# A decoder kernel: the heads' copy ahead of the exponentials, grouped loads at the opening, table products in two pairs, and two key and value units ahead of the barrier

## The reference, cut to what matters

```python
x = _layernorm(x + L0_attn(x))            # block-diagonal gates and a decaying scan
x = _layernorm(x + L0_xattn(x, ctx, ctx)) # retention: rotated q, k, a decay mask
x = _layernorm(x + L0_ffn(x))             # mixture of experts: 8 experts, top 2, 1024 slots each
x = _layernorm(x + L1_attn(x))            # causal self-attention, 2 heads of 128, rope, softmax
x = _layernorm(x + L1_xattn(x, ctx))      # 16 heads of 16 over ctx, with biases and a mask
x = _layernorm(x + L1_ffn(x))             # hashed experts, top 4 of 64

# L0_ffn: every token goes to its expert's slot and comes back by it
disp = disp.at[topi, pos_c].add(xk)
h = relu(einsum('ecm,emh->ech', disp, w1) + b1);  y = einsum('ech,ehm->ecm', h, w2) + b2
out = sum(gate[..., None] * y[topi, pos_c], axis=1)

# L1_xattn: keys and values hang on ctx alone
K = key_value_input @ Wk + bk;  V = key_value_input @ Wv + bv
```

## Time and profile before

| | |
|---|---|
| median of 3 runs | 1661.8 us (1661.14 to 1669.12) |
| the profiled execution | 1667.65 us, span 1665.9 us |
| TensorE clock granted, mean | 0.977 |
| PE busy | 1527.8 us, 92% of the span |
| PE weight loads, beside it | 1364.2 us, 82% |
| DVE busy | 1140.6 us, 68% |
| ACT busy | 801.7 us, 48% |
| POOL busy | 578.7 us, 35% |
| bytes moved | 152.03 MB, mean 91 GB/s |

### The profile page before, as it was taken

The page is one execution under the profiler, slowest core; times in us unless marked ns, Lnnn a source line. Parts: engine busy times, 40 slices in busy tenths (PEclk is TensorE's granted clock), DMA queues, the critical chain, the costliest instruction groups (busy, mean ns, idle before and its releaser), DMA issues.

```text
span 1665.9 us, 34482 instructions
## 1 busy us (share of the span) xinstructions
PE 1527.8 (92%) x12806; PEld 1364.2 (82%) x12806; DVE 1140.6 (68%) x2334; ACT 801.7 (48%) x1527; POOL 578.7 (35%) x679
## 2 busy tenths in 40 slices
PE   3888898899999999788888699999989999999997
PEld 2677777799999999777777578888879999999997
DVE  3899987756655565146777358877867768676775
ACT  5777742244544455236666444545434444443443
POOL 2666651212112120047776211212104444343444
PEclk8999999899999999999999899999999999999999
DMA  5122253212323330152233132121134553635443
GB/s 188 64 77 76 70 189 115 83 39 89 96 95 101 101 102 26 49 200 74 77 91 96 65 124 77 53 78 53 53 73 93 104 121 83 123 85 110 97 92 72
DMA packets 118829, 152.03 MB, mean 91 GB/s; under 512 B 10330, under 2 KB 103716, under 8 KB 118180
## 3 DMA queue, kind: packets, MB, share of 16 engines
q1 hardware_dynamic: 111540, 129.75, 28.4%
q0 software_dynamic: 6144, 16.79, 3.6%
q10 hardware_dynamic: 1008, 3.67, 0.6%
HBM read 111.37 MB, written 38.80 MB: 90 GB/s over the span
## 4 chain that ended last, share of the span: by engine, by line
PE 29%; DVE 11%; issue 7%; DMA 5%; ACT 4%; SPq 1%; POOL 1%; DVEq 0%; ACTq 0%; POOLq 0%
PE psum L518 7%; PE psum L1788 4%; DMA arena_x<-wT_d 3%; PE psum L1772 3%; PE psum L485 3%; PE psum L493 2%; PE psum L1766 2%; DVE psum L2358 2%; PE psum L1749 2%; PE psum L1488 1%; ACT arena_y L1519 1%; DMA wT_d<-arena_w 1%; DVE C_st L437 1%; PE psum L477 1%; PE psum L1485 1%
## 5 line engine op out<-in xcount | busy, mean ns | idle before, releaser
L2129 POOL TENSOR_TENSOR d_g_parts<-arena_w,d_g_parts 128x512 fp32r<-128x512 f32 x128 | 167.8, 1311 | 248.6 <-ACT d_g_parts L2261 240.9
L518 PE MATMUL psum<-d_v_high,d_g_parts 128*128 128x256 f32 x1024 | 205.1, 284 | 4.0 <-POOL d_g_parts L2129 2.3
L518 PE MATMUL psum<-d_x_parts,d_v_high 128*128 128x256 f32 x1024 | 193.5, 287 | 1.7 <-DVE d_x_parts L513 1.7
L518 PE MATMUL psum<-m_w_high,m_h_parts 128*128 128x256 f32 x1024 | 188.0, 285 | 0.0
L1192 ACT ACTIVATE arena_x<-psum,b_e 128x512 f32<-128x512 f32 x128 | 88.2, 689 | 190.1 <-PE psum L518 90.7
L518 PEld LDWEIGHTS psum<-d_v_high,d_g_parts 128*128 128x128 f32 x1024 | 167.5, 190 | 6.5 <-POOL d_g_parts L2129 4.1
L1120 POOL DMA_INDIRECT arena_x<-x_d,slot_row x64 | 66.9, 1045 | 293.6 <-PE psum L1166 229.3
L518 PEld LDWEIGHTS psum<-d_x_parts,d_v_high 128*128 128x128 f32 x1024 | 159.0, 191 | 8.6 <-DVE arena_w L2364 4.1
L518 PE MATMUL psum<-m_xF_parts,m_w_high 128*128 128x512 f32 x512 | 160.2, 395 | 2.1 <-DVE m_xF_parts L513 2.1
L518 PEld LDWEIGHTS psum<-m_w_high,m_h_parts 128*128 128x128 f32 x1024 | 160.9, 192 | 0.0
L2261 ACT ACTIVATE d_g_parts<-arena_w 128x512 fp32r<-128x512 f32 x128 | 80.8, 631 | 153.3 <-DVE arena_w L2364 152.4
(11 more groups left out here) (279 smaller groups left out, 3694.0 us busy)
## 6 DMA issues: line engine op xcount, KB each, us to landing
arena_x<-wT_d SPq DMA_DIRECT2D x128, 256.0 KB, 6.4
arena_y<-in_L_ffn_w SPq DMA_DIRECT2D x16, 1024.0 KB, 7.9
x_d<-arena_x SPq DMA_DIRECT2D x32, 256.0 KB, 2.2
y_d<-arena_x SPq DMA_DIRECT2D x16, 512.0 KB, 9.0
arena_x<-kv_d SPq DMA_DIRECT2D x16, 512.0 KB, 3.3
kv_d<-arena_x SPq DMA_DIRECT2D x9, 512.0 KB, 3.0
arena_x<-in_x SPq DMA_DIRECT2D x16, 256.0 KB, 2.9
arena_x<-in_ctx SPq DMA_DIRECT2D x16, 256.0 KB, 3.2
```

Source lines behind the costliest of these rows:

```text
L518: ins = nc.tensor.matmul(dst, left[a_], right[b_], start=start and k == 0, stop=stop and k == 2, skip_group_check=True)
L2129: nc.gpsimd.tensor_tensor(K["gP"][:, s % 4, 1], K["g"][:, s % 2], K["gP"][:, s % 4, 0].bitcast(F32), ALU.subtract).then_inc(d_gl, 1)
```

## The change

1. **Opening.** SP issues first the identity (128 x 128 of the constants), then x of unit 0, the vectors and the mask, then eight of the diagonal blocks; ACT issues the other eight, ahead of its first table load; POOL issues the rest of the constants, the three weights and the routing weight, through its software queue. There are four semaphores instead of one: `s_const`, `s_diag`, `s_tables`, `s_weights`. DVE's chain to `ndecay` comes ahead of what A doesn't need at once; three operations that need tables go to DVE's step 2.
2. **Routing.** Parts 0 and 1 of the table products follow ctx unit 5, parts 2 and 3 unit 6 (before: 0 behind unit 5, 1 behind 6, 2 and 3 behind 7). `KV_FIRST` is 10 instead of 9: one unit more is projected there.
3. **The barrier and C's start.** Four of the six remaining ctx units are loaded during M. Two are projected behind M's last tile, ahead of the barrier (ACT copies them; their stores are issued behind it). Three are projected ahead of C's step 0, and the last in step 3.
4. **C.** The heads' copy stands ahead of the exponentials in `c_scalar`.

```diff
-        loads = [(const[:, :], a["constants"])]
+        loads, tables_in, weights_in = [], [(const[:, P:], a["constants"][:, P:])], []
...
-            loads.append((w[name][:, :, :], a[name].rearrange("(c p) n -> p c n", p=P)))
-        loads.append((w_route[:, :, :], a["L0_ffn_wg"].rearrange("(c p) n -> p c n", p=P)))
+            weights_in.append((w[name][:, :, :], a[name].rearrange("(c p) n -> p c n", p=P)))
+        weights_in.append((w_route[:, :, :], a["L0_ffn_wg"].rearrange("(c p) n -> p c n", p=P)))
         loads.append((mask_in[:, :], a["mask"]))
-        N_EARLY = len(loads) + len(diag)
+        N_EARLY = 1 + len(loads)
...
         def setup_sync(sp):
+            sp.dma_start(const[:, 0:P], a["constants"][:, 0:P]).then_inc(s_const, 16)
+            sp.dma_start(A["x"][:, 0], x_u[0]).then_inc(a_in[0], 16)
             for dst, src in loads:
                 sp.dma_start(dst, src).then_inc(s_const, 16)
             sp.wait_ge(s_zero, 1)
-            for dst, src in diag:
-                sp.dma_start(dst, src).then_inc(s_const, 16)
+            for dst, src in diag[::2]:
+                sp.dma_start(dst, src).then_inc(s_diag, 16)
 
         def setup_pool(pool):
             nc.gpsimd.memset(gate_w[:, :, :, :], 0.0).then_inc(s_zero, 1)
             nc.gpsimd.memset(pool_cell[:, :], 0.0).then_inc(s_pow, 1)
             nc.gpsimd.memset(minus_half[:, :, :], -0.5).then_inc(s_pow, 1)
             pool.wait_ge(s_pow, 2)
+            for dst, src in tables_in:
+                pool.dma_start(dst, src).then_inc(s_tables, 16)
+            for dst, src in weights_in:
+                pool.dma_start(dst, src).then_inc(s_weights, 16)
 
         def setup_scalar(act):
-
+            act.wait_ge(s_zero, 1)
+            for dst, src in diag[1::2]:
+                act.dma_start(dst, src).then_inc(s_diag, 16)
             act.wait_ge(s_vec, 1)
...
         def setup_vector(dve):
             dve.wait_ge(s_const, 16 * N_EARLY)
             nc.vector.tensor_scalar(mask_f[:, :], mask_in[:, :], -BIG, None, ALU.mult).then_inc(s_maskf, 1)
-            dve.wait_ge(s_maskT, 1)
-            nc.vector.tensor_copy(mask_key[:, :], bank(6)[:, 0:B]).then_inc(s_mask, 1)
             dve.wait_ge(s_vecT, 1)
             nc.vector.tensor_copy(vec[:, :], bank(7)[:, 0:VEC_ROWS]).then_inc(s_vec, 1)
             dve.wait_ge(s_vec, 1)
             nc.vector.tensor_scalar(hgate_b[:, :], vec[:, V_BIN:V_BIN + 4], 0.5, None, ALU.mult).then_inc(s_setup, 1)
+            nc.vector.tensor_scalar(ndecay[:, :], vec[:, V_A:V_A + 2], 0.0, MIN_DECAY, ALU.max,
+                                    ALU.add).then_inc(s_setup, 1)
+            dve.wait_ge(s_maskT, 1)
+            nc.vector.tensor_copy(mask_key[:, :], bank(6)[:, 0:B]).then_inc(s_mask, 1)
+            dve.wait_ge(s_act_setup, 3)
+            dve.wait_ge(s_setup, 2)
+            nc.vector.tensor_tensor(ndecay[:, :], ndecay[:, :], sp_tmp[:, 2, :], ALU.add).then_inc(s_setup, 1)
+            dve.wait_ge(s_setup, 3)
+            nc.vector.tensor_scalar(pdecay[:, :], ndecay[:, :], 0.5, None, ALU.mult).then_inc(s_setup, 1)
+            dve.wait_ge(s_setup, 4)
+            nc.vector.tensor_scalar(ndecay[:, :], ndecay[:, :], -0.5, None, ALU.mult).then_inc(s_setup, 1)
+            nc.vector.memset(mask_one[:, :], -BIG).then_inc(s_setup, 1)
+            nc.vector.tensor_copy(ident_bf[:, :], ident).then_inc(s_setup, 1)
+
+        def setup_tables(dve):
+            dve.wait_ge(s_tables, 16)
             nc.vector.tensor_scalar(kb_par[:, 0, :], vec[:, V_BK:V_BK + 2], table("even_heads"), None,
                                     ALU.mult).then_inc(s_setup, 1)
             nc.vector.tensor_scalar(kb_par[:, 1, :], vec[:, V_BK:V_BK + 2], table("odd_heads"), None,
                                     ALU.mult).then_inc(s_setup, 1)
-            nc.vector.tensor_scalar(ndecay[:, :], vec[:, V_A:V_A + 2], 0.0, MIN_DECAY, ALU.max,
-                                    ALU.add).then_inc(s_setup, 1)
-            nc.vector.tensor_copy(ident_bf[:, :], ident).then_inc(s_setup, 1)
             nc.vector.tensor_copy(causal_bf[:, :], table("causal")).then_inc(s_setup, 1)
-            nc.vector.memset(mask_one[:, :], -BIG).then_inc(s_setup, 1)
-            dve.wait_ge(s_act_setup, 3)
-            dve.wait_ge(s_setup, 4)
-            nc.vector.tensor_tensor(ndecay[:, :], ndecay[:, :], sp_tmp[:, 2, :], ALU.add).then_inc(s_setup, 1)
-            dve.wait_ge(s_setup, 8)
-            nc.vector.tensor_scalar(pdecay[:, :], ndecay[:, :], 0.5, None, ALU.mult).then_inc(s_setup, 1)
-            dve.wait_ge(s_setup, 9)
-            nc.vector.tensor_scalar(ndecay[:, :], ndecay[:, :], -0.5, None, ALU.mult).then_inc(s_setup, 1)
+
+        N_DECAY = 5
         N_SETUP = 10
...
+                if u0 and not (u0.fixed and u0.n == 0):
...
+                    if t.fixed and t.n == 1:
+                        pe.wait_ge(s_diag, 16 * len(diag))
...
+                    if t.fixed and t.n == 4:
+                        pe.wait_ge(s_weights, 16 * len(weights_in))
...
-            act.wait_ge(s_setup, N_SETUP)
+            act.wait_ge(s_setup, N_DECAY)
...
+                    setup_tables(dve)
...
+                        pool.wait_ge(s_tables, 16)
...
-        KV_FIRST = 9
+        KV_FIRST, KV_LAST, KV_AHEAD, KV_EMPTY = 10, 2, 4, 5
...
                 if n == 5:
                     r_slot_rows(pe, 0)
+                    r_slot_rows(pe, 1)
                 if n == 6:
-                    r_slot_rows(pe, 1)
-                if n == 7:
                     r_slot_rows(pe, 2)
...
+        KV["cF_ahead"] = arena_x.shaped(arena_x.tile[:, 18432:20480], [P, KV_AHEAD, NC_, T])
...
+                if t.fixed and t.n == TILES - 1:
+                    done(sp, m_yp, Unit(0, TILES - 3))
+                    for k in range(KV_AHEAD):
+                        sp.dma_start(KV["cF_ahead"][:, k].rearrange("p c t -> p (c t)"),
+                                     cF_d[KV_FIRST + k]).then_inc(kv_ahead, 16)
...
+        KV["kv_rest"] = arena_x.shaped(arena_x.tile[:, 13312:17408], [P, 4, 2, NC_ * T])
+        kl_p, kl_s = sem("kl_p"), sem("kl_s")
+
+        def kv_last_tensor(pe):
+            pe.wait_ge(kv_ahead, 16 * KV_AHEAD)
+            for k in range(KV_LAST):
+                project_features(bank(4 - 2 * k), "L1_xattn_Wk", KV["cF_ahead"][:, k])
+                project_rows(bank(5 - 2 * k), "L1_xattn_Wv", KV["cF_ahead"][:, k]).then_inc(kl_p, 1)
+
+        def kv_last_scalar(act):
+            for k in range(KV_LAST):
+                act.wait_ge(kl_p, k + 1)
+                for j in range(2):
+                    nc.scalar.activation(KV["kv_rest"][:, k, j], bank(4 - 2 * k + j), ACT.Copy).then_inc(kl_s, 1)
+
+        add("tensor", kv_last_tensor)
+        add("scalar", kv_last_scalar)
+
         def m_end(sp):
             for k in range(2):
                 sp.wait_ge(m_st[k], 16 * (TILES // 2))
+            sp.wait_ge(kl_s, 2 * KV_LAST)
...
+        def kv_rest_project(pe, k):
+            if k < KV_AHEAD:
+                src = KV["cF_ahead"][:, k]
+            else:
+                src = KV["cF_rest"][:, k - KV_AHEAD]
+                pe.wait_ge(kr_in[k - KV_AHEAD], 16)
+            done(pe, kr_s, Unit(0, k - KV_LAST - 2), 2)
+            project_features(bank(4 + 2 * (k % 2)), "L1_xattn_Wk", src)
+            project_rows(bank(5 + 2 * (k % 2)), "L1_xattn_Wv", src).then_inc(kr_p, 1)
+
+        def kv_rest_take(act, k):
+            act.wait_ge(kr_p, k - KV_LAST + 1)
+            landed4(act, kr_st, Unit(0, k - 4, 4))
+            for j in range(2):
+                nc.scalar.activation(KV["kv_rest"][:, k % 4, j], bank(4 + 2 * (k % 2) + j),
+                                     ACT.Copy).then_inc(kr_s, 1)
+            act.wait_ge(kr_s, 2 * (k - KV_LAST + 1))
+            kv_rest_store(act, k)
+
+        def kv_rest_store(act, k):
+            act.dma_start(kv_d[KV_FIRST + k], KV["kv_rest"][:, k % 4]).then_inc(kr_st[k % 4], 16)
 
         def c_sync(sp):
             def step(t):
-                if t.fixed and t.n < 2:
-                    for k in ((0, 1), range(2, KV_REST))[t.n]:
-                        kv_rest_load(sp, k)
+                if t.fixed and t.n == 2:
+                    for k in range(KV_REST - KV_AHEAD):
+                        sp.dma_start(KV["cF_rest"][:, k].rearrange("p c t -> p (c t)"),
...
         def c_tensor(pe):
-            kv_rest_tensor(pe)
+            for k in range(KV_LAST, KV_EMPTY):
+                kv_rest_project(pe, k)
...
+                if t.fixed and t.n == 3:
+                    for k in range(KV_EMPTY, KV_REST):
+                        kv_rest_project(pe, k)
+                    pe.wait_ge(kr_s, 2 * (KV_REST - KV_LAST))
...
         def c_scalar(act):
-            kv_rest_scalar(act)
+            for k in range(KV_LAST):
+                kv_rest_store(act, k)
+            for k in range(KV_LAST, KV_EMPTY):
+                kv_rest_take(act, k)
 
             def step(t):
```

(11 more changed lines are left out.)

33 lines of the change are left out of this document (7 added, 26 removed).

## The result

Measured together, 20 runs each: before 1671.46 us, after 1658.73 us (medians; one run of before took 8529 us, which moves no median); ratio 0.9935, 95% interval 0.9917 to 0.9954. That is some 11 us less by the ratio (12.7 between the medians) where 26 were forecast, and 1658.73 lies above the range of 1625 to 1649. The direction was right, the size less than half. The median of before was itself 10 us above the 1661.8 of the three runs shown first; where that comes from is told under "All together". On the base of 1661.8, on which the range stands, the ratio gives 1651.0, still above 1649.

A forecast was written before the change was run, and what follows sets the result against it. PE busy 92% of the span; DVE bounds phase A, with waits at the opening, M's start, C's start and C's rounds. Terms -7.8, -2.0, -6.1, -7.6, -2.8 sum to -26.3: median forecast 1635.5 us, range 1625 to 1649.

The forecast's parts named there:

- The opening: Kernel's start: fewer SP loads ahead of the diagonal blocks let PE start earlier, -7.8 us, bounds -8.7 and -5.
- the third rival: Opening: small loads land behind 2.2 MB of tables, PE starts at 12.2, saving 3 us instead of 7.8; chance 0.08.
- I take 7.3: Opening: PE's assumed start in us, 6.5 being the earliest, against 15.19 before.
- The slower rival: Opening: POOL writes the descriptors of five large loads itself and is slow; 1694 us at k = 4; chance 0.03.
- The routing: Routing and M's start: first turn 0.3 us later but at a higher clock, -2.0 us, bounds +0.6 and -3.2.
- My bound of +0.6: Routing and M's start: the slow end, in us, of the bounds on the -2.0 term.
- C's start: Barrier and C's start: ACT normalises 11.6 us earlier, less 5.5 for clock and step 3: -6.1 us, bounds -11 and -3.
- forecast +5.5: C's start, behind the normalising: +2.5 us for PE's lower clock and +3.0 for the sixth unit in step 3.
- The second rival: C's start gives nothing: barrier, step 3, clock and memory-bound gathers take the gain, 1641.6 us; chance 0.14.
- The rounds and the last round: C: the earlier heads' copy saves 0.69 us in each of 11 rounds, -7.6 us, and -2.8 in the last round.
- the new circle: C's rounds: the chain through q and values that bounds a round after the copy's move, 11.86 us against 12.55.
- The first rival: C's rounds don't get shorter, the circle still closing at 12.5 us: 1644.4 us; chance 0.16.

The follow-up runs named there:

- opening_held: Kernel before with the new opening alone, POOL issuing tables and weights only when all sixteen diagonal blocks have landed; ratio 0.9926.
- the six combined profiles: Changed kernel with POOL's loads held, table products in old places, two late ctx loads first, in four unit placings, two of them run twice; ratios to before 0.9825 to 0.9884.
- after_spaced: Changed kernel with the four parts of the table products in their old places; ratio to before 0.9917.
- copy_only: Kernel before with only the heads' copy moved ahead of the exponentials; ratio 0.9955.
- combined: Changed kernel with POOL's loads held until the diagonal blocks landed, table products in old places, two late ctx loads first; ratio to before 0.9884, run again 0.9840.
- the last four kernels: Changed kernel with loads held, old table-product places and early ctx loads, in four placings of the six units, on one chip; ratios to before 0.9825 to 0.9840.
- after_early_cF: Changed kernel with SP issuing the two late ctx loads of C's start first, in step 0; ratio to before 0.9899.

## Why the prediction was wrong

**The opening: a term mis-sized, by the third rival.** Forecast -7.8 with PE at 7.3; measured -3.1 in after and -3.6 to -5.3 in the five other profiles of this opening, with PE at 10.9 to 11.9. The step that failed is "I take 7.3": it counted issues and the landing of an undisturbed load. The rival that let the small loads come in behind 2.2 MB gave -3 and was right, in its mechanism too; I gave it 0.08. With the bytes held back the term is -8.7 in opening_held, -8.6 to -8.9 in five of the six combined profiles and -6.5 in one, so the rest of the working stands. The slower rival, POOL's own time, was far off: 0.75 us for a load, whatever its size here, where I had 6 us for five at the least.

**The routing: a wrong sign.** Forecast -2.0, measured +4.1. I moved part 1 of the table products directly behind part 0 and wrote the 0.9 us for which PE waits there, but asked of the clock only at M's start, where the change could help. At the new wait I put it at nothing. There the clock fell, and 5.1 us on PE came right where the extra unit had made PE the last to be ready: the turn followed ACT's copy (1.18 idle), not the gathers. My bound of +0.6 left that out. The rest of the term was sound: without the fall it is -1.5.

**C's start: a wait that I didn't look for.** Forecast -6.1. The 3.7 us for the barrier were right (gathers begin 10.4 us behind M's last sums, before 6.6, +3.8), and so was what comes behind the normalising: forecast +5.5, measured 36.9 - 30.3 = 6.6. Wrong was "ACT is free (three units of PE end at 717.5), so it normalises" at 722.2: five units need five loads, four were ahead, and the fifth was queued on SP behind 1 MB of others. It was at 729.4. That the first mix came 1.5 us later than I had it is the rest. This part of the loss varies, too: the same kernel had 64.9, and after_spaced, with the load in the same place, 62.6. And the placing itself is worth little. Two ahead of the barrier and one in step 3 give 63.5, 62.7 and 62.7 us where the loads are first, all six at C's start 64.7, 62.0 and 62.7. The old placing gives 67.1 to 68.9 in seven profiles. The one unit that moved to the routing, 3.46 us, can be most of that difference; that is an estimate, since no run moves it alone, nor the four loads that are now issued in M. The second rival, "C's start gives nothing", had the right outcome for this kernel, but a late load was not among its reasons.

**The rounds and the last round: right.** 12.55 to 11.81 us, as the new circle said (11.86), and -12.2 for all of C's rounds where -7.6 - 2.8 = -10.4 were forecast: the 11 rounds gained 8.1, and what stands behind them 4.1. I had priced there only the last round, while three of the last four intervals gain, 1.1 to 1.7 us each. The first rival is out: copy_only shows 169.1 us.

**What was in no term.** +3.9 and +3.2 us in E and the last phase. The kernel before took 28.3 and 32.4 us for E's start, so the 32 doesn't need the change; whether the new order of the copy makes it more frequent (13 of 13, against 3 of 5 at 31.9 or more) stays open. The +3.2 lies within the long level of the last phase: 692.2 and 693.4 us with the old opening and placing, 694.4 to 695.4 in the seven others. Whether the change adds 1 to 3 us there stays open as well; at the short level no such difference shows. Without these two stretches the profiled pair gives -3.1 + 4.1 + 1.1 - 12.2 = -10.1, near the 11 of the ratio, where its spans differ by 2.9; that they agree so well is in part luck, since after's profile was the slowest of its 20 runs.

The three large errors went one way because each part was priced by what it takes off a chain, and what it adds to a shared resource (the tables' bytes, the clock at the new wait, SP's queue ahead of the fifth load) was priced at nothing. With the three removed, the sum of the forecast is there: combined has -8.6 - 0.8 - 4.4 - 12.2 = -26.0 us in the first four stretches, and the last four kernels have ratios of 0.9825 to 0.9840; the forecast's was 0.9842 (their medians are 1638.8 to 1644.2 us, the forecast was 1635.5). That it fits so closely is luck: term by term the forecast was -7.8, -2.0, -6.1 and -10.4.

## What to carry to other kernels

When loads are spread over more issuing engines to free one of them, order them by bytes as well: what the first instruction needs must land before the large ones are issued, not only be issued first. When work is moved ahead of a wait, list for each moved piece the load that it needs and where that stands in its queue. And a short new wait on the matrix engine can cost several us behind it through the clock (here 5.1 us behind a wait of 0.85), so look at each wait that a rearrangement creates, and not only at those that it removes. Where a profile shows a stretch shorter, ask which of the edits stands in that stretch: most of what after_early_cF gained stood in another.

## What the runs showed that I had not expected

- A plain load issued by POOL took it 0.74 to 0.78 us, for 8 KB as for 1404 KB.
- The clock fell to its lower level behind a wait of only 0.85 us, in 4 of 5 profiled executions, with table products (128x65, 0.11 us apart at full clock) ahead of it. The same products with a unit of 128x256 products between them and no wait (parts 0 and 1 apart) kept the higher level in all 13.
- The last phase has two levels, 10 us apart, by which DVE's waits for `wT_d` are 22 or 45 us, in one and the same kernel.
